# Mixers: ScalarE's copy of the first sequence's turned gated rows, one place forward, in front of the squares of the sixth head

## The chip, the cores and the metric

The kernel runs on one NeuronCore of one Trainium2 chip. The metric is the device time of one execution in microseconds (us); lower is better. The engines named below are TensorE (PE, with its weight loads PEld), VectorE (DVE), ScalarE (ACT), GpSimd (POOL) and SyncE (SP). Each engine works through its own instructions in order and waits for others on semaphores.

## The reference, cut to what matters

The program is a decoder of two layers over 8 sequences of 256 tokens, 512 wide. The part around the change is the second layer's first mixer, a Mamba2 block with four heads, and the cross attention behind it:

```
y = _ssd(x, dt, A, Bm, Cm) + D[None, None, :, None] * x
g = y.reshape(b, l, D_INNER) * jax.nn.silu(z)
gr = g.reshape(b, l, NHEADS, HEADDIM)
rstd = jax.lax.rsqrt(jnp.mean(gr * gr, axis=-1, keepdims=True) + 1e-05)
yn = (gr * rstd).reshape(b, l, D_INNER) * norm_w
return yn @ out_proj_w.T
...
x = x + _L1_attn_ref(_layernorm(x, axis=-1), ...)
x = x + _L1_xattn_ref(_layernorm(x, axis=-1), ctx_2048, ctx_2048, L1_xattn_gamma)
```

Each head's gated rows are squared and summed, scaled by the reciprocal root of their mean square, and all four heads together are multiplied with the output weights. The result, added to `x`, is normalized again and goes into the cross attention.

## The kernel before, in words

The function `mixers` takes the 8 sequences in four pairs, `first` and `second`. Tokens of a sequence lie in two tiles of 128 rows (`NT` is 2, `P` is 128), the 512 columns in four chunks of 128, one for each head (`MH` is 4). The order of each engine's instructions is written out by hand in one block for each engine; semaphores join them. Nothing is planned or scheduled by a program.

The 8 heads of a pair (heads 0 to 3 of the first sequence, 4 to 7 of the second) pass through a loop over `k` on every engine. For one head:

- TensorE's `decays` (L2137 to L2145) builds the decays and the products of B and C in PSUM banks 0 to 3, two of each in turn; `outputs` (L2156 to L2158) multiplies the weights with the inputs.
- ScalarE's `decays` (L1989) takes the exponential of the decays, VectorE's `weights` (L2378) multiplies it with the products, VectorE's `gated` (L2386, L2390) adds the skip and multiplies with the gate and writes `y`.
- ScalarE's `squares` (L1995) squares the head's two row tiles and sums them, GpSimd's `gate_norm` (L1880, L1881) raises the mean to the power of minus a half, and ScalarE's `scaled` (L2004) multiplies `y` with it.

In its round `k` ScalarE issues `decays(k)`, `scaled(k - 3)` and `squares(k - 2)`. The last scaling of a sequence counts `attn_ready` up. TensorE's `turn_gated` (L2096) waits for it, turns 128x128 blocks of `y` by eight multiplications with the identity, into banks 0 and 1, and counts `rowsT_psum` up. Since these banks hold the decays of the last heads, TensorE waits, before it turns the first sequence, until ScalarE has taken the exponential of the eighth head; then it issues `outputs` of the eighth head, and then `project_out(first, j)`:

```
if k == 2 * MH:
    pe.wait_ge(sy["decay_ready"], k0 + k)
    turn_gated(first)
if k >= 1:
    outputs(k0 + k - 1)
...
for j in range(NT):
    project_out(first, j)
turn_gated(second)
project_out(second, 0)
```

ScalarE's `gated_copy` (L1930) copies the turned blocks from banks 0 and 1 into `hT`, one instruction for each bank, and counts `colsT_ready`. `project_out` (the multiplications are in the helper `project_pe`, L188) waits until both copies are done; its first part is the one of the first sequence, for the two row tiles one after the other. Behind it VectorE adds the residual (L2397), takes the statistics (L2301, L2302), GpSimd takes the reciprocal root (L174, L175), VectorE applies it (L2307), ScalarE and VectorE split the rows in two parts (`high` L2010, `low` L2410), and TensorE starts the scores of the cross attention (`scores`, L2178). ScalarE's `context_high(second)` (L1967), a copy of 128x1024, stands between the last scaling of the second sequence and its `gated_copy`. The cross attention takes 32 rounds, and then the next pair begins.

Of the kernel before, what the change touches and what calls it, by code (L numbers as in the profile page):

```python
# [1664 lines left out]
MH = 4  # L1665
# [28 lines left out]
def mixers(nc, sy, const, dr, tiles, nseq=NSEQ):  # L1694
# [3 lines left out]
    with ExitStack() as ctx:  # L1698
# [71 lines left out]
        def dt_calls(p):  # L1770

            n = NT * MH
            return ((0, n), (n, 2 * n)) if p == 0 else ((0, 2 * n),)

        def dt_count(s):

            return s + 1 if s < 2 else s // 2 + 2
# [139 lines left out]
        def _(act):  # L1917
            def rows_copy(s):
                b = s % 2
                for j in range(NT):  # L1920
                    act.wait_ge(sy["rowsT_psum"], 8 * (s // 2) + NT * b + j + 1)
                    act.activation(hT[b][:, :, j * P:(j + 1) * P],
                                   bank(2 * b + j).rearrange("p (c t) -> p c t", c=KC), ACT.Copy
                                   ).then_inc(sy["colsT_ready"], 1)

            def gated_copy(s):
                b = s % 2
                for j in range(NT):
                    act.wait_ge(sy["rowsT_psum"], 8 * (s // 2) + 4 + NT * b + j + 1)
                    act.activation(hT[b][:, :, j * P:(j + 1) * P], bank(j).rearrange("p (c t) -> p c t", c=KC), ACT.Copy  # L1930
                                   ).then_inc(sy["colsT_ready"], 1)

            def time_steps(at, end, count):
                act.wait_ge(sy["dtabs_ready"], count)
                act.activation(dts[:, 2, at:end], dts[:, 1, at:end], ACT.Exp, scale=-1.0).then_inc(sy["dtexp_ready"], 1)
                act.wait_ge(sy["dtone_ready"], count)
                act.activation(dts[:, 4, at:end], dts[:, 3, at:end], ACT.Ln).then_inc(sy["dtln_ready"], 1)

            def convolved(seqs):
                chunks = [NXBC * s + c for s in seqs for c in range(NXBC)]  # L1940
                for n in chunks + [chunks[-1] + 1]:
                    if n <= chunks[-1]:
                        b, c = (n // NXBC) % 2, n % NXBC
                        act.wait_ge(sy["xbc_psum"], n + 1)
                        act.activation(convh[b][:, c, :], bank(1 + n % 3)[:, 0:S], ACT.Identity,
                                       bias=conv_b[:, c:c + 1], scale=conv_w[:, c, 3:4])
                        act.activation(raw[b][:, c, :], bank(1 + n % 3)[:, 0:S], ACT.Copy).then_inc(sy["xbc_raw_ready"], 1)
                    if n > chunks[0]:
                        b, c = ((n - 1) // NXBC) % 2, (n - 1) % NXBC
                        act.wait_ge(sy["conv_ready"], n)  # L1950
                        if n >= 3:
                            act.wait_ge(sy["xbc_ready"], n - 2)
                        act.activation(cth[:, (n - 1) % 2, :], convh[b][:, c, :], ACT.Tanh
                                       ).then_inc(sy["convtanh_ready"], 1)

            def gates(s):
                b = s % 2
                if s >= 2:
                    act.wait_ge(sy[f"mixed_out{b}"], 16 * (s // 2))
                for j in range(NT):  # L1960
                    act.wait_ge(sy["z_psum"], NT * s + j + 1)
                    act.activation(xz[b][:, j, :], bank(4 + 2 * b + j), ACT.Tanh, scale=0.5
                                   ).then_inc(sy["ztanh_ready"], 1)

            def context_high(s):
                act.wait_ge(sy["cx_in"], 16 * (s + 1))
                act.activation(cx2[s % 2][0][:], cx[:], ACT.Copy).then_inc(sy["cx_hi_ready"], 1)  # L1967

            def input_rows(s):
                b = s % 2  # L1970
                act.wait_ge(sy["xrows_psum"], s + 1)
                act.activation(xr[b], bank(4 + b)[:, S:2 * S].rearrange("p (t d) -> p t d", t=NT), ACT.Copy
                               ).then_inc(sy["xrows_ready"], 1)

            def scaled_rows(s):
                b = s % 2
                act.wait_ge(sy["xrows_ready"], s + 1)
                act.wait_ge(sy["dA_ready"], dt_count(s))
                for t in range(NT):
                    for hd in range(MH):  # L1980
                        at = (b * NT + t) * MH + hd
                        ins = act.activation(xdt[b][:, t, hd, :], xr[b][:, t, :], ACT.Copy, scale=dts[:, 8, at:at + 1])
                ins.then_inc(sy["xdt_ready"], 1)

            def decays(k):
                act.wait_ge(sy["decay_psum"], k + 1)
                if k >= 2:
                    act.wait_ge(sy["w_ready"], k - 1)
                act.activation(decay[:, k % 2, :], bank(k % 2)[:, 0:3 * P], ACT.Exp).then_inc(sy["decay_ready"], 1)  # L1989

            def squares(k):
                b, hd = (k // MH) % 2, k % MH
                act.wait_ge(sy["gated_ready"], k + 1)
                for j in range(NT):
                    ins = act.activation(h[b][:, j, hd * P:(hd + 1) * P], y[b][:, j, hd * P:(hd + 1) * P], ACT.Square,  # L1995
                                         accum_out=ssq[b][:, j * MH + hd:j * MH + hd + 1])
                ins.then_inc(sy["sumsq_ready"], 1)

            def scaled(k):
                b, hd = (k // MH) % 2, k % MH  # L2000
                act.wait_ge(sy["gated_norm"], k + 1)
                for j in range(NT):
                    head = y[b][:, j, hd * P:(hd + 1) * P]
                    ins = act.activation(head, head, ACT.Copy, scale=grstd[b][:, j * MH + hd:j * MH + hd + 1])  # L2004
                    if hd == MH - 1:
                        ins.then_inc(sy["attn_ready"], 1)
# [6 lines left out]
            def copy_recips(s, g):  # L2013
                act.wait_ge(sy["recT_psum"], NT * s + g + 1)
                act.activation(y[s % 2][:, g, :], bank(7 - g), ACT.Copy, scale=gamma).then_inc(sy["rec_ready"], 1)
# [20 lines left out]
            for p in range(npair):  # L2036
                first, second = 2 * p, 2 * p + 1
                if p == 0:
                    for s in (first, second):
                        rows_copy(s)  # L2040
                        time_steps(*dt_calls(0)[s], dt_count(s))
                        convolved((s,))
                else:
                    time_steps(*dt_calls(p)[0], dt_count(first))
                    convolved((first, second))
                context_high(first)
                gates(first)
                gates(second)
                input_rows(first)
                input_rows(second)  # L2050
                scaled_rows(first)
                k0 = 2 * MH * p
                for k in range(2 * MH + 3):
                    if k < 2 * MH:
                        decays(k0 + k)
                    if k == 1:
                        scaled_rows(second)
                    if k >= 3:
                        scaled(k0 + k - 3)
                    if 2 <= k < 2 * MH + 2:  # L2060
                        squares(k0 + k - 2)
                    if k == 2 * MH:
                        gated_copy(first)
                context_high(second)
                gated_copy(second)
                for j in range(NT):
                    high(first, j)
                q0 = HP * p
                for i in range(HP + 3):
                    if i < HP:  # L2070
                        exponentials(q0 + i)
                    if 1 <= i <= HP:
                        turned_copy(q0 + i - 1)
                    if i in (8, 9):
                        high(second, i - 8)
                    if i in (11, PAIRS + 11):
                        copy_recips(first + i // PAIRS, 0)
                    if i in (PAIRS + 2, HP + 2):
                        copy_recips(first + i // PAIRS - 1, 1)
                    if p + 1 < npair and i in (HP + 1, HP + 2):  # L2080
                        rows_copy(first + 2 + i - HP - 1)
# [1055 lines left out]
```

## Time and profile before

| what | value |
|---|---|
| time, median of 3 runs | 3378.61 us (3377.27 to 3384.95) |
| span of the profiled execution | 3330.3 us |
| median time less this span | 48.3 us |
| busy share of PE, DVE, ACT, POOL | 92%, 70%, 48%, 24% |

The span goes from the first to the last instruction of one profiled execution. That execution has no device time of its own beside its span here, so the 48.3 us around the span are taken from the median of the three timed runs. Busy shares are averages over stages with different limits. The mixers take the stretch from 1875 to 2656 us of the span; the four pairs' head loops end near 2013, 2198, 2375 and 2546 us.

### The profile page before, as it was taken

How to read it: one execution, taken by the hardware profiler on the slowest of the kernel's cores; microseconds unless marked ns; L12 is line 12 of the kernel's file. 1: busy time of each engine (PE TensorE's matmuls, PEld its weight loads, DVE VectorE, ACT ScalarE, POOL GpSimd, SP SyncE). 2: the span in 40 equal slices, each digit the busy share in tenths (PEclk: the TensorE clock that was granted, in tenths of full speed). 3: DMA queues.
4: the chain of work that ended last, by engine and by line, in shares of the span. 5: the costliest groups of instructions: out<-in, count | busy, mean ns of one | idle time of the engine just before them, and what ended most of it. 6: DMA issues, size and time to landing. Idle time of an engine off the chain costs nothing. (4 is left out here: it accounts for less than half of the span.)

```text
span 3330.3 us, 61582 instructions
## 1 busy us (share of the span) xinstructions
PE 3071.3 (92%) x22897; PEld 2479.2 (74%) x22897; DVE 2317.9 (70%) x4413; ACT 1596.5 (48%) x3648; POOL 805.7 (24%) x1000
## 2 busy tenths in 40 slices
PE   7999999997999799999999769889899889999999
PEld 5666666664888688888888656667576578888888
DVE  4655665564766588888888667868686777777776
ACT  3323333332221455555555336566575655555555
POOL 1221122121554111111111143432323012222222
PEclk9999999998999899999999979999999989999999
DMA  6324332321121677777777621311110132222222
GB/s 260 127 93 148 109 127 102 115 102 39 28 57 34 206 247 241 244 243 240 241 247 248 235 59 58 97 62 54 36 61 7 40 113 78 70 74 73 70 74 70
DMA packets 145099, 401.95 MB, mean 121 GB/s; under 512 B 39200, under 2 KB 48032, under 8 KB 131952
## 3 DMA queue, kind: packets, MB, share of 16 engines
q1 hardware_dynamic: 106448, 323.37, 28.6%
q0 software_dynamic: 18976, 50.45, 5.2%
q10 hardware_dynamic: 19456, 25.18, 2.2%
q8 instruction: 141, 2.31, 0.3%
q14 instruction: 78, 0.64, 0.1%
HBM read 344.16 MB, written 54.76 MB: 120 GB/s over the span
## 5 line engine op out<-in xcount | busy, mean ns | idle before, releaser
L1470 POOL DMA_INDIRECT xg<-normed_rows,idx x128 | 125.4, 979 | 662.5 <-PE psum L1552 590.0
L2655 POOL TENSOR_TENSOR mixf<-act 128x256 f32<-128x256 f32 x128 | 143.5, 1121 | 497.8 <-DVE act L2916 497.8
L174 POOL TENSOR_SCALAR ve<-mv 128x1 f32<-128x1 f32 x112 | 34.9, 311 | 841.0 <-DVE mv L780 575.5
L1567 PE MATMUL psum<-xT_hi,wgu_hi 128*128 128x192 f32 (+1 forms) x1536 | 228.8, 271 | 4.2 <-ACT aT_lo L1534 4.2
L1567 PE MATMUL psum<-xT_lo,wgu_hi 128*128 128x192 f32 (+1 forms) x1536 | 223.2, 268 | 0.0
L1567 PE MATMUL psum<-xT_hi,wgu_lo 128*128 128x192 f32 (+1 forms) x1536 | 223.0, 267 | 0.0
L1606 DVE TENSOR_TENSOR wgu_lo<-wgu,wgu_hi 128x1408 fp32r<-128x1408 f32 x128 | 202.5, 1623 | 22.9 <-ACT wgu_hi L1494 22.8
L1567 PEld LDWEIGHTS psum<-xT_hi,wgu_hi 128*128 128x128 f32 (+1 forms) x1536 | 191.1, 183 | 28.8 <-ACT wgu_hi L1494 21.5
L1507 ACT ACTIVATE eth<-psum 128x192 f32<-128x192 f32 (+1 forms) x192 | 63.2, 329 | 298.7 <-PE psum L1567 298.7
L2024 ACT ACTIVATE scratch<-psum,smin 128x512 f32<-128x512 f32 x256 | 173.7, 685 | 62.8 <-DVE smin L2416 60.6
L1567 PEld LDWEIGHTS psum<-xT_lo,wgu_hi 128*128 128x128 f32 (+1 forms) x1536 | 190.8, 183 | 0.0
L1567 PEld LDWEIGHTS psum<-xT_hi,wgu_lo 128*128 128x128 f32 (+1 forms) x1536 | 190.7, 183 | 0.0
L2416 DVE TENSOR_REDUCE smin<-psum 128x2 f32<-128x1024 f32 x128 | 155.4, 1217 | 34.0 <-PE psum L2178 33.2
L1494 ACT ACTIVATE wgu_hi<-wgu 128x1408 fp32r<-128x1408 f32 x128 | 169.5, 1379 | 18.7 <-DMA wd<-in_w_d_dram 18.7
L2916 DVE TENSOR_TENSOR act<-act,maskT 128x512 f32<-128x512 f32 x128 | 88.2, 689 | 116.9 <-ACT act L2693 116.9
L2188 PEld LDWEIGHTS psum<-ident,scratch 128*128 128x128 f32 x1024 | 108.9, 141 | 59.4 <-issue 38.2
L2188 PE MATMUL psum<-ident,scratch 128*128 128x128 f32 x1024 | 144.8, 281 | 8.1 <-DVE scratch L2423 4.9
L1640 DVE SCALAR_TENSOR_TENSOR eact<-eth,psum 128x192 f32<-128x192 f32 (+1 forms) x192 | 67.5, 352 | 108.9 <-ACT eth L1507 107.1
L2926 DVE TENSOR_TENSOR ca_lo<-act,ca_hi 128x512 fp32r<-128x512 f32 x128 | 134.4, 1050 | 12.5
L558 PE MATMUL psum<-hT_hi,w_slot 128*128 128x256 f32 x768 | 113.5, 292 | 12.3 <-ACT hT_hi L468 5.9
L1053 POOL DMA_INDIRECT slot_token<-tok_i,slot_w x96 | 102.5, 1068 | 77.3 <-DVE slot_r L1337 52.2
L902 DVE TENSOR_SCALAR arena<-psum,hi 128x512 f32<-128x512 f32 x128 | 87.3, 745 | 43.9 <-PE psum L672 43.9
(431 smaller groups left out, 8681.1 us busy)
## 6 DMA issues: line engine op xcount, KB each, us to landing
wgu<-in_w_gu_dram SPq DMA_DIRECT2D x64, 1408.0 KB, 6.1
w_slot<-w_split SPq DMA_DIRECT2D x21, 2048.0 KB, 7.8
wd<-in_w_d_dram SPq DMA_DIRECT2D x64, 512.0 KB, 8.7
w_raw<-in_w_dram SPq DMA_DIRECT2D x128, 256.0 KB, 2.6
expert_out<-yo ACTq DMA_DIRECT2D x64, 256.0 KB, 5.2
w_slot<-w_split SPq DMA_DIRECT2D x28, 512.0 KB, 4.9
wd<-in_w_d_dram SPq DMA_DIRECT2D x64, 192.0 KB, 9.0
w_split<-w_slot SPq DMA_DIRECT2D x4, 2048.0 KB, 9.0
```

The costliest lines, as they stand in the source:

```text
L558: ins = pe.matmul(out, lhs_of(lp, kc), rhs_of(rp, kc), start=(m == 0 and kc == 0), stop=(m == 2 and kc == KC - 1))
L1053: pool.indirect_dma_start(out=dr["slot_token"], out_offset=bass.IndirectOffsetOnAxis(ap=slot_w[s % 2][:, j, k:k + 1], axis=0), in_=tok_i[s ...
L1470: pool.indirect_dma_start(out=xg[b][0:w, t, :], out_offset=None, in_=rows, in_offset=bass.IndirectOffsetOnAxis(ap=idx[b][0:w, t:t + 1], ax ...
L1494: act.activation(wgu2[b][0][:, gu], wgu[b][:, gu], ACT.Copy).then_inc(sy["wgu_hi"], 1)
L1567: ins = pe.matmul(bank(2 + m)[0:w, gu * CAP:(gu + 1) * CAP], wgu2[b][wp][:, gu, kc, m0:m0 + w], xT2[b][xp][:, kc, :], start=(i == 0 and kc ...
L1606: dve.tensor_tensor(wgu2[b][1][:, gu], wgu[b][:, gu], wgu2[b][0][:, gu].bitcast(F32), ALU.subtract).then_inc(sy["wgu_lo"], 1)
L2024: act.activation(prob[:, q % 4, k, :], bank_pair(2 * (q % 2))[:, k, :], ACT.Exp, bias=smin[b][:, n, k:k + 1], scale=-1.0, accum_out=ssum[b ...
L2188: ins = pe.transpose(bank(4 + k)[:, mc * P:(mc + 1) * P], prob[:, q % 4, k, mc * P:(mc + 1) * P], ident)
L2416: dve.tensor_reduce(smin[(q // PAIRS) % 2][:, q % PAIRS, :], bank_pair(2 * (q % 2)), AX.X, ALU.min).then_inc(sy["smin_ready"], 1)
L2655: pool.tensor_tensor(mixf[:, g % LAG, :], act2[:, g % LAG, 0, :], act2[:, g % LAG, 1, :], ALU.add).then_inc(sy["f_mix"], 1)
L2916: dve.tensor_tensor(act2[:, g % LAG], act2[:, g % LAG], maskT[(g // FC) % 2][:, 2:4, :], ALU.mult).then_inc(sy["f_ca"], 1)
L2926: dve.tensor_tensor(ca2[1][:, g % LAG], act2[:, g % LAG], ca2[0][:, g % LAG].bitcast(F32), ALU.subtract).then_inc(sy["f_ca_lo"], 1)
```

## The change

ScalarE's `gated_copy(first)` moves in the last rounds of the head loop. It stood in round `k == 8` behind `scaled` of head 5 and `squares` of head 6 (heads counted from 0). It now stands in round `k == 7`, behind `scaled` of head 4 and ahead of `squares` of head 5, the sixth head. No instruction is added or removed, and no other engine's order is touched.

```diff
                     if k >= 3:
                         scaled(k0 + k - 3)
+                    if k == 2 * MH - 1:
+                        gated_copy(first)
                     if 2 <= k < 2 * MH + 2:
                         squares(k0 + k - 2)
-                    if k == 2 * MH:
-                        gated_copy(first)
                 context_high(second)
                 gated_copy(second)
```

On ScalarE, at the end of the first pair's head loop, the order changes as follows (the same piece stands in each of the four pairs; L1989 is `decays`, L2004 `scaled`, L1995 `squares`, L1930 `gated_copy`):

```order
 L1989 ACTIVATE decay<-psum 128x384
 L2004 ACTIVATE y<-y,grstd 128x128 x2
-L1995 ACTIVATE h,ssq<-y 128x128 x2
-L2004 ACTIVATE y<-y,grstd 128x128 x2
-L1995 ACTIVATE h,ssq<-y 128x128 x2
 L1930 ACTIVATE hT<-psum 128x4x128 x2
+L1995 ACTIVATE h,ssq<-y 128x128 x2
+L2004 ACTIVATE y<-y,grstd 128x128 x2
+L1995 ACTIVATE h,ssq<-y 128x128 x2
 L2004 ACTIVATE y<-y,grstd 128x128 x2
 L1995 ACTIVATE h,ssq<-y 128x128 x2
```

The copy passes two pairs of squarings and one pair of scalings.

On TensorE, which waits for this copy and is waited for by it, the same place in the first pair reads thus before and after alike (L2096 is `turn_gated`, L2156 to L2158 `outputs` of the eighth head, L188 `project_out`, L2178 the first scores):

```order
L2096 MATMUL psum<-ident,y 128x128 x8
L2156 MATMUL psum<-scratch,wgt 128x128
L2157 MATMUL psum<-scratch,wgt 128x128
L2158 MATMUL psum<-scratch,wgt 128x128
L188 MATMUL psum<-w_mo,hT 128x512 x8
L2096 MATMUL psum<-ident,y 128x128 x8
L188 MATMUL psum<-w_mo,hT 128x512 x4
L2178 MATMUL psum<-cx_hi,h_hi 128x512 x2
```

Nothing moved here. The profile counts each of these L188 multiplications twice (16 and 8 records), and the three of L2156 to L2158 as six.

## Rows read from the trace of the kernel before

**Rows 1.** The page's head and its busy line.

```profile
span 3330.3 us, 61582 instructions
PE 3071.3 (92%) x22897; PEld 2479.2 (74%) x22897; DVE 2317.9 (70%) x4413; ACT 1596.5 (48%) x3648; POOL 805.7 (24%) x1000
```

**Rows 2.** Line L1930: who waited for the copies, all pairs.

```profile
L1930 ACT ACTIVATE hT<-psum x16: 572/584/597, 2016.1 to 2560.9; 128x512 f32<-128x512 f32 x16
...
  PE psum L188: 19.0, 8
```

**Rows 3.** Timeline, first pair: start, length, engine, line, [idle before, releaser].

```profile
2011.42 1.09 PE L2096 MATMUL psum<-ident,y 128*128 128x128 f32 x8 [1.15 <-ACT decay L1989]
...
2012.08 0.69 ACT L2004 ACTIVATE y<-y,grstd 128x128 f32<-128x128 f32 x2 [0.71 <-POOL grstd L1881]
...
2012.80 0.39 PE L2158 MATMUL psum<-scratch,wgt 128*128 128x128 f32 x2
...
2013.03 0.31 ACT L1995 ACTIVATE h<-y 128x128 f32<-128x128 f32 x1 [0.26 <-DVE y L2390]
...
2014.90 0.69 ACT L2004 ACTIVATE y<-y,grstd 128x128 f32<-128x128 f32 x2 [1.17 <-POOL grstd L1881]
2015.50 0.29 ACT L1995 ACTIVATE h<-y 128x128 f32<-128x128 f32 x1
...
2016.08 1.05 ACT L1930 ACTIVATE hT<-psum 128x512 f32<-128x512 f32 x2
...
2016.54 0.69 POOL L1881 TENSOR_TENSOR grstd<-ssq,minus_half 128x2 f32<-128x2 f32 x1
...
2017.19 9.91 PE L188 MATMUL psum<-w_mo,hT 128*128 128x512 f32 x16 [4.01 <-ACT hT L1930]
2017.26 0.69 ACT L2004 ACTIVATE y<-y,grstd 128x128 f32<-128x128 f32 x2
```

**Rows 4.** Windows, first pair: stretch; busy by engine; PEclk.

```profile
2015.00:2016.00 1.00, 0.00 (x0) 0.00 (x0) 0.09 (x1) 1.00 (x6) 0.00 (x0) 0.99 0.00 0
2016.00:2017.20 1.20, 0.01 (x1) 0.01 (x1) 0.00 (x0) 1.14 (x4) 0.85 (x2) 0.50 0.00 0
2017.20:2022.20 5.00, 5.00 (x6) 2.17 (x7) 0.00 (x0) 2.92 (x9) 0.90 (x3) 0.50 0.02 3
2024.00:2026.50 2.50, 2.50 (x7) 1.07 (x6) 0.39 (x1) 0.00 (x0) 0.00 (x0) 1.00 0.00 0
```

**Rows 5.** Timeline, first pair, behind the gap: the second sequence's way.

```profile
2019.62 0.69 ACT L2004 ACTIVATE y<-y,grstd 128x128 f32<-128x128 f32 x2 [1.08 <-POOL grstd L1881]
...
2020.22 1.04 ACT L1967 ACTIVATE cx_hi<-cx 128x1024 fp32r<-128x1024 f32 x1
...
2026.93 1.04 PE L2096 MATMUL psum<-ident,y 128*128 128x128 f32 x8
...
2027.57 1.08 ACT L1930 ACTIVATE hT<-psum 128x512 f32<-128x512 f32 x2 [6.31 <-PE psum L2096]
...
2028.71 3.70 PE L188 MATMUL psum<-w_mo,hT 128*128 128x512 f32 x8 [0.74 <-ACT hT L1930]
...
2031.14 1.48 DVE L2410 SCALAR_TENSOR_TENSOR h_lo<-h,h_hi 128x512 fp32r<-128x512 f32 x2
...
2032.34 0.52 PE L2178 MATMUL psum<-cx_hi,h_hi 32*128 32x512 f32 x4
```

**Rows 6.** Timeline of PE, pairs two and four, first projection and the turning behind it.

```profile
2201.95 9.69 PE L188 MATMUL psum<-w_mo,hT 128*128 128x512 f32 x16 [4.01 <-ACT hT L1930]
2211.48 1.04 PE L2096 MATMUL psum<-ident,y 128*128 128x128 f32 x8
...
2550.30 9.59 PE L188 MATMUL psum<-w_mo,hT 128*128 128x512 f32 x16 [4.01 <-ACT hT L1930]
2559.73 1.04 PE L2096 MATMUL psum<-ident,y 128*128 128x128 f32 x8
```

**Rows 7.** Windows at the start of pairs two and three, columns as in rows 4.

```profile
2132.00:2134.00 2.00, 2.00 (x11) 2.00 (x12) 0.00 (x0) 0.00 (x0) 0.51 (x1) 0.51 0.02 2
2312.00:2314.00 2.00, 2.00 (x11) 1.77 (x10) 0.40 (x3) 1.97 (x4) 0.25 (x1) 1.00 0.05 4
```

**Rows 8.** Timeline of VectorE's first two weights, pairs three and four.

```profile
2354.08 1.01 DVE L2378 TENSOR_TENSOR wgt<-decay,psum 128x384 f32<-128x384 f32 x2
2359.80 0.56 DVE L2378 TENSOR_TENSOR wgt<-decay,psum 128x384 f32<-128x384 f32 x1 [4.70 <-PE psum L2145]
...
2527.45 1.02 DVE L2378 TENSOR_TENSOR wgt<-decay,psum 128x384 f32<-128x384 f32 x2 [2.55 <-ACT decay L1989]
2530.84 0.55 DVE L2378 TENSOR_TENSOR wgt<-decay,psum 128x384 f32<-128x384 f32 x1 [2.37 <-PE psum L2145]
```

## The prediction

> **What bounds the kernel now.** I read the page first: TensorE is busy for 92% of the span and no other engine for more than 70% [rows 1]. An average over 3330 us says little of a change at four places, so the next view is the line of the copy itself. TensorE waited 19.0 us in eight waits for the copies of L1930 [rows 2]. The timelines split this sum: four waits of 4.01 us for the first sequence's copy [rows 3, 6] and four of 0.74 us for the second's [rows 5], 16.04 + 2.96 = 19.0 us. So the places to look at are the four gaps of 4.01 us.
>
> The timeline around the first gap shows what TensorE lacks. It has turned the rows by 2012.51 (2011.42 + 1.09) and ended the eighth head's outputs by 2013.19 (2012.80 + 0.39). The copy of the turned rows starts only at 2016.08, not because its input is late, but because it stands in ScalarE's queue behind the squares of head 5, its scaling, and the squares of head 6; and that scaling itself stood 1.17 us for GpSimd's power [rows 3]. The projection starts at 2017.19.
>
> The gap has a second price. The granted clock was full until about 2016.0, 2.8 us after the last matmul, and then 0.50, the 1.2 GHz level; it was still 0.50 from 2017.2 to 2022.2, under dense matmuls, and full again from 2024 [rows 4]. In the first pair the 16 records of the projection take 2026.93 - 2017.19 = 9.74 us from its start to the next turning [rows 3, 5]. The same multiplication at the full clock, 8 records of the second sequence, takes 2032.34 - 2028.71 = 3.63 us to the scores that follow it [rows 5]. Twice that is 7.26 us and counts the start and end of a group twice; I take 7.1 us for 16. So the slow clock costs 9.74 - 7.1 = 2.6 us in pair one. In pairs two and four the stretch is 9.53 and 9.43 us [rows 6] (pair three repeats pair two), 2.4 and 2.3 us over 7.1.
>
> **The change part by part.** Nothing is removed or added: two copies of 584 ns in each pair [rows 2], issued earlier.
>
> *When the copy can start.* It now stands behind the scaling of head 4, which starts at 2012.08. When nothing is waited for, ScalarE's next instruction follows a pair of scalings after 0.60 us (2014.90 to 2015.50) [rows 3], so the copy comes up at 2012.68. Its input: for the second sequence the first copy starts 0.64 us after the turning starts (2026.93 to 2027.57) [rows 5], here 2011.42 + 0.64 = 2012.06, and the last turning ends by 2012.51. Both banks are thus ready and I put the wait at nothing. From the other side: if the second bank follows the first by half of the turning (0.55 us), it is ready at 2012.06 + 0.55 = 2012.61, which is still ahead of 2012.68.
>
> *When the projection can start.* From the copies' start to the projection are 2017.19 - 2016.08 = 1.11 us [rows 3]. 2012.68 + 1.11 = 2013.79, instead of 2017.19: 3.40 us earlier. The eighth head's outputs end at 2013.19, so TensorE is free, and its gap shrinks from 4.01 to 0.60 us.
>
> *The clock.* A gap of 0.60 us behind a stretch in which the clock stayed full through gaps of 1.15 us [rows 3] should leave it full: 2.6 us in pair one on top, and the turning of the second sequence can start at 2013.79 + 7.1 = 2020.9 instead of 2026.93.
>
> *What is pushed back.* The squares of head 5 waited for VectorE until 2013.03. They now stand behind the copies, which hold ScalarE for about 1.0 us (they last 1.05 us together, and a following instruction starts a little before the end), that is until 2013.68: 0.65 us late. Behind them are queued: GpSimd's power for head 5, the scaling of head 5, the squares of head 6, and so on to the scaling of head 7 and the context copy. The copy no longer stands between the squares of head 6 and the scaling that now starts at 2017.26, but nothing is won there, since GpSimd's power ends at 2016.54 + 0.69 = 2017.23 anyway [rows 3]. So the 0.65 us stay: the scaling of head 7 starts at 2020.27 instead of 2019.62 and ends at about 2020.96, the context copy starts at 2020.87 instead of 2020.22 and ends at 2021.91 [rows 5]. TensorE turns from 2020.9; its first four blocks need only the first of the two scaled tiles, so this delay, if it shows, is under 0.1 us. Before, it had about 6.6 us of slack.
>
> *What is late next.* The second sequence's copy waits for the turning (2020.9 + 0.64 = 2021.5) and for ScalarE, which is in the context copy until 2021.9. So it starts at 2021.9, held by ScalarE, instead of 2027.57: 5.67 us earlier. Its projection follows 1.14 us later, as before (2027.57 to 2028.71) [rows 5]: 2023.0 for 2028.71. Of the 2.6 us that the clock gives, 0.35 us are thus lost again to the context copy.
>
> *What follows.* The scores start when this projection ends, if the split rows are there. Before, the second part of the split starts by the end of the first at about 2031.88 (2031.14 and half of 1.48), 0.46 us ahead of TensorE's 2032.34 [rows 5]. That chain hangs on the first sequence's projection, which ends 3.40 + 2.6 = 6.0 us earlier, so its slack grows to 0.8 us. The scores start 5.7 us earlier, and from there on everything, the 32 rounds and the next pair, hangs on these starts and moves along. GpSimd's gathers and the loads are started by counts of the same loop.
>
> *The sum.* In pair one the copy starts 2021.9 - 2017.19 = 4.71 us after the projection's old start; before it started 10.38 us after it (2027.57 - 2017.19). In the other pairs the old figure is the turning's start and 0.64 us: 9.53 + 0.64 = 10.17 twice, 9.43 + 0.64 = 10.07 [rows 6]. The gains are 5.67 + 5.46 + 5.46 + 5.36 = 21.95 us. The span goes from 3330.3 to 3308.3 us. The median of the runs shown is 48.3 us above the span, and I keep that distance: 3378.6 - 22.0 = 3356.6 us.
>
> *What the shift may do elsewhere.* The clock also falls at other places, and not in each pair. At the start of pair two it was 0.51, at the same place of pair three 1.00 [rows 7]; and from the first weights of the head loop to the third are 2359.80 - 2354.08 = 5.72 us in pair three and 2530.84 - 2527.45 = 3.39 us in pair four, which kept its clock [rows 8]. So one such fall costs up to 2.3 us, and a shift by some us can make or save it.
>
> A rule of the skill bears on this. The Trainium skill, page "TensorE: Matmul & The Clock Gate", section "What's actually happening", says that the monitor behind the gate runs freely, so that where the clock changes depends on when the work arrives, not only on what it is. The differences between pairs in rows 7 and 8 agree. By that rule the shift can cost or give several us at places that the change does not touch; what that would make here is the third rival below.
>
> **The rivals.**
>
> *The clock falls all the same.* The transposes and short heads ahead of the gap may count for too little. For it: it fell in all four pairs. Against it: it stayed full through 1.15 us gaps, and fell only 2.8 us after the last matmul. Then the gain is the 3.40 us of the gap alone, carried through turning and copy: 13.6 us, 3365.0 us. Chance 9%.
>
> *The rounds behind do not move.* If the end of a pair were set by something that the copy does not start, such as the gathers or the context's low part on GpSimd, the gap's gain would be waited away: 3378.6 us. Against it: GpSimd is busy 24% [rows 1] and its work there is started by the rounds' own counts. Chance 4%.
>
> *The clock falls elsewhere more often.* At 2.3 us each [rows 8], three falls more take 6.9 us back: 15.1 us of gain, 3363.5 us. Two falls fewer give 4.6 us on top: 3352.0 us. Chance of a shift of 3 us or more either way 15%, still faster.
>
> *ScalarE stands at the copy.* The other side. The copy now heads the queue of squares, scalings and the context copy; if the turned rows came late, all of these and the second sequence's turning would wait. What TensorE waits for before it turns is the exponential of the eighth head, which ScalarE issues ahead of the scaling of head 4, so the wait worked out is nothing. It decides only from a wait of about 6 us on, where the slack of 6.6 us of the second's turning is used up; a wait of 8 us would cost about 2 us a pair: 3386 us. Chance 3%.
>
> **How the numbers follow.** The forecast as worked out, within 3 us, has 69%; the rivals have 9, 4, 15 and 3%. The predicted time is 3356.6 us. The range reaches to the better bound, 3351, and takes in the rival of the clock, 3365, with a margin: 3351 to 3366. A measurement of this kernel tells 0.2%, 6.8 us, from no change. Only the second rival and part of small remainders end within that: 4%; slower 3%; faster 93%.
>
> **What would show it right or wrong.** In the profile after: the L188 waits for L1930 sum to about 4 x 0.6 + 4 x 1.1 = 7 us instead of 19.0. The first projection begins about 0.6 us behind the outputs of the eighth head, and its 16 records show no 0.50 clock. The second's copy begins right behind the context copy, without idle time. The scaling of head 7 is 0.65 us later against the exponential of head 7. ScalarE's idle time before the first copy is nothing. If the clock row shows 0.50 behind the shorter gap, or ScalarE idles before the first copy, that step was wrong; if all of these hold and the span is not about 22 us shorter, the loss lies in the rounds behind or in falls of the clock at other places.

## The result, and the profile after

| | kernel before | changed kernel |
|---|---|---|
| median | 3379.99 us (3377.27 to 3384.95, 4 runs) | 3353.63 us (3351.07 to 3361.1, 4 runs) |
| ratio | | 0.9923, 95% interval 0.9911 to 0.9935 |

The change makes the kernel 26.4 us faster by the medians, 22 to 30 us by the interval. The forecast was 22.0 us.

The first pair in the trace of the changed kernel, timeline, to be laid beside [rows 3] and [rows 5]:

```profile
2023.37 1.09 PE L2096 MATMUL psum<-ident,y 128*128 128x128 f32 x8 [1.15 <-ACT decay L1989]
2024.02 0.69 ACT L2004 ACTIVATE y<-y,grstd 128x128 f32<-128x128 f32 x2 [0.71 <-POOL grstd L1881]
2024.62 1.06 ACT L1930 ACTIVATE hT<-psum 128x512 f32<-128x512 f32 x2
...
2025.58 0.30 ACT L1995 ACTIVATE h<-y 128x128 f32<-128x128 f32 x1
2025.74 7.13 PE L188 MATMUL psum<-w_mo,hT 128*128 128x512 f32 x16 [0.61 <-ACT hT L1930]
...
2027.41 0.69 ACT L2004 ACTIVATE y<-y,grstd 128x128 f32<-128x128 f32 x2 [1.15 <-POOL grstd L1881]
...
2032.13 0.69 ACT L2004 ACTIVATE y<-y,grstd 128x128 f32<-128x128 f32 x2 [1.08 <-POOL grstd L1881]
2032.71 1.04 PE L2096 MATMUL psum<-ident,y 128*128 128x128 f32 x8
2032.73 1.04 ACT L1967 ACTIVATE cx_hi<-cx 128x1024 fp32r<-128x1024 f32 x1
...
2033.68 1.06 ACT L1930 ACTIVATE hT<-psum 128x512 f32<-128x512 f32 x2
2034.79 3.70 PE L188 MATMUL psum<-w_mo,hT 128*128 128x512 f32 x8 [1.05 <-ACT hT L1930]
...
2036.92 1.47 DVE L2410 SCALAR_TENSOR_TENSOR h_lo<-h,h_hi 128x512 fp32r<-128x512 f32 x2
...
2038.42 0.52 PE L2178 MATMUL psum<-cx_hi,h_hi 32*128 32x512 f32 x4
```

The copy starts 0.60 us behind the scaling of head 4, without idle time. TensorE's gap is 0.61 us instead of 4.01. The 16 records of the projection take 2032.71 - 2025.74 = 6.97 us to the next turning instead of 9.74. The second copy starts right behind the context copy. From the first turning to the scores are 15.05 us instead of 20.92.

The waits of TensorE for the copies are 6.6 us instead of 19.0 [rows 2]:

```profile
  PE psum L188: 6.6, 8
```

The windows of the same stretch, columns as in [rows 4], show the clock full throughout:

```profile
2025.00:2028.00 3.00, 2.39 (x8) 1.07 (x7) 1.97 (x8) 1.85 (x8) 0.95 (x2) 1.00 0.00 0
2028.00:2033.00 5.00, 5.00 (x15) 2.31 (x14) 0.78 (x2) 2.83 (x14) 1.76 (x4) 1.00 0.00 0
```

Worked out in the same way for each pair, first turning to first scores, in us:

| pair | before | changed | difference |
|---|---|---|---|
| 1 | 20.92 | 15.05 | 5.87 |
| 2 | 20.70 | 15.06 | 5.64 |
| 3 | 20.71 | 15.05 | 5.66 |
| 4 | 20.61 | 15.06 | 5.55 |

Together 22.7 us. This takes the first trace of the kernel before as the measure; a second trace of it (`base`, below) has 81.1 us at the four places where the first has 82.9, and against it the gain is 20.8 us. The rest of the trace cannot be compared so simply: the changed kernel's profiled execution has a longer span (3359.1 us) than the one of before [rows 1], though the changed kernel is faster by the clocked runs. The section on the hardware comes back to this.

### The profile page after: what moved, and what is told of

Read it like the earlier page. It is cut to its first block and busy times, and to the rows that moved or that the text cites. A ratio compares the mean times of both kernels' runs of the same rounds, so it can differ in the third digit from the quotient of the medians.

```text
span 3359.1 us, 61582 instructions
## 1 busy us (share of the span) xinstructions
PE 3100.1 (92%) x22897; PEld 2500.8 (74%) x22897; DVE 2317.4 (69%) x4413; ACT 1596.6 (48%) x3648; POOL 801.4 (24%) x1000
## 5 line engine op out<-in xcount | busy, mean ns | idle before, releaser
L2188 PE MATMUL psum<-ident,scratch 128*128 128x128 f32 x1024 | 154.1, 292 | 10.1 <-issue 4.7
L558 PE MATMUL psum<-hT_hi,w_slot 128*128 128x256 f32 x768 | 113.1, 291 | 12.2 <-ACT hT_hi L468 5.8
```

The source lines that it names most:

```text
L2188: ins = pe.transpose(bank(4 + k)[:, mc * P:(mc + 1) * P], prob[:, q % 4, k, mc * P:(mc + 1) * P], ident)
```

## The experiments

Four sets of runs were made, and each is compared with runs of the kernel before on its own device: medians 3331.90 us (the first four kernels), 3331.91 us (the next four), 3382.02 us (`control`, `heads23`, `ctx23`), 3388.25 us (`base`). The second set has no run of the changed kernel itself, so its kernels are laid beside it by the ratio. "Local" is the sum over the four pairs of the stretch from turning to scores, against the 82.9 us of before.

| kernel | median us | ratio to before, 95% interval | local us |
|---|---|---|---|
| `again` | 3314.26 | 0.9945, 0.9932 to 0.9959 | -22.7 |
| `warm` | 3325.94 | 0.9983, 0.9974 to 0.9992 | -10.3 |
| `behind` | 3319.66 | 0.9967, 0.9955 to 0.9979 | -20.1 |
| `ctx` | 3312.37 | 0.9942, 0.9928 to 0.9955 | -24.0 |
| `gapback` | 3333.54 | 1.0002, 0.9992 to 1.0013 | -4.0 |
| `early` | 3313.08 | 0.9933, 0.9915 to 0.9952 | -22.7 |
| `split` | 3313.48 | 0.9941, 0.9926 to 0.9956 | -26.1 |
| `heads` | 3318.14 | 0.9954, 0.9937 to 0.9971 | -22.7 |
| `control` | 3355.73 | 0.9930, 0.9914 to 0.9946 | -22.7 |
| `heads23` | 3355.64 | 0.9927, 0.9913 to 0.9941 | -22.7 |
| `ctx23` | 3352.94 | 0.9921, 0.9907 to 0.9935 | -24.0 |
| `base` | 3387.44 | 0.9996, 0.9981 to 1.0012 | -1.9 |

**`again`**: the changed kernel, unchanged.

> The changed kernel once more. Theory (the four gaps and the clock inside them): the stretch from the first turning to the second sequence's projection is 11.4 us in each pair, as in its first trace, against 17.29, 17.07, 17.08 and 16.97 us before, 22.7 us in all, and the time is 22 to 23 us under the kernel before. Rival (the change also gives something elsewhere, since 3353.6 against 3380.0 us is 26.4 us): the time is 25 us or more under it again, and the trace shows further stretches of the mixers that are shorter. The 2060 to 2068 us stretch of the first trace, where TensorE, VectorE and ScalarE stood idle behind a fetch, either comes back (then it belongs to the new order) or does not.

The four places are 15.06 us each, as in the first trace. The gain is 17.6 us by the medians, 13.7 to 22.7 us by the interval: smaller than the first time, and less than the 22 to 23 us expected. The idle stretch at 2060 us did not come back.

**`warm`**: the order of before, and work of no use in TensorE's gap.

```diff
+                for n in range(4):
+                    pe.matmul(bank(2), ident, w_mo[:, n, :], start=True, stop=True)
                 for j in range(NT):
                     project_out(first, j)
```

> The kernel before, with the copy in its old place, and four multiplications of no use by TensorE in the gap of 4.01 us, so that its clock is kept. Theory (the gap costs twice, by itself and by the clock behind it): the gap keeps its end, the projection's 16 records take 7.0 us instead of 9.4 to 9.7, and the time is about 10 us under the kernel before (2.8 + 2.6 + 2.6 + 2.5). Rival (the clock is no part of it, or falls all the same): no change, within 2 us.

The timeline of TensorE in pair one (L2261 is the filling):

```profile
2014.27 1.09 PE L2096 MATMUL psum<-ident,y 128*128 128x128 f32 x8 [1.15 <-ACT decay L1989]
...
2015.86 3.60 PE L2261 MATMUL psum<-w_mo,ident 128*128 128x512 f32 x8
2020.04 7.13 PE L188 MATMUL psum<-w_mo,hT 128*128 128x512 f32 x16 [0.58 <-ACT hT L1930]
2027.01 1.04 PE L2096 MATMUL psum<-ident,y 128*128 128x128 f32 x8
```

The projection starts 5.77 us behind the turning, exactly as before, and yet takes 6.97 us instead of 9.74. So the low clock behind the gap came from the gap, and filling it takes 10.3 us off the four places. The time fell by 3 to 9 us, less than that. Against the second trace of before, whose four places are 1.9 us shorter, the local gain is 8.5 us, which the interval (up to 8.7 us) still holds. The mechanism holds; whether part of its gain is given back elsewhere is not shown by this run alone.

**`behind`**: the copy one place later than in the changed kernel.

```diff
                     if 2 <= k < 2 * MH + 2:
                         squares(k0 + k - 2)
-                    if k == 2 * MH:
+                    if k == 2 * MH - 1:
                         gated_copy(first)
```

> The copy one place later than in the changed kernel, behind the squares of head 5 and ahead of round 8. Theory: the first copy starts 0.9 us later than in the changed kernel, TensorE's gap is 1.5 us, its clock stays full, the squares of head 5 are not pushed back, and the second sequence's copy is held by the turning, no more by the context copy: 0.6 us a pair, 2.4 us in all slower than the changed kernel, about 20 us under the kernel before. Rival (the clock falls behind a gap of 1.5 us): about 12 us under the kernel before.

```profile
2013.72 1.09 PE L2096 MATMUL psum<-ident,y 128*128 128x128 f32 x8 [1.15 <-ACT decay L1989]
2014.38 0.69 ACT L2004 ACTIVATE y<-y,grstd 128x128 f32<-128x128 f32 x2 [0.71 <-POOL grstd L1881]
...
2015.93 1.06 ACT L1930 ACTIVATE hT<-psum 128x512 f32<-128x512 f32 x2
...
2017.05 7.13 PE L188 MATMUL psum<-w_mo,hT 128*128 128x512 f32 x16 [1.56 <-ACT hT L1930]
```

As expected: a gap of 1.56 us, and still 6.97 us for the projection, so the clock stays full. Locally it is 2.6 us behind the changed kernel. By the times it is 5.4 us behind `again`, more than the local difference, and only 12.2 us under the kernel before (7 to 15 us by the interval), where about 20 were expected. That is the figure of the rival, the fall of the clock, though the trace shows none at the four places: the time alone would have named the wrong cause. It is also the clearest case of a local gain (20.1 us, or 18.2 us against `base`) that the time does not show in full.

**`ctx`**: the context copy behind the second gated copy.

```diff
-                context_high(second)
                 gated_copy(second)
+                context_high(second)
```

> The changed kernel with ScalarE's context copy of the second sequence moved behind the second sequence's gated copy. Theory: the second copy then waits for the turning alone and starts 0.33 us earlier in each pair, 1.3 us in all. Rival (the context copy is then late for what follows, or the split rows hold the scores): no change or slower.

The second copy waits 0.51 us for the turning now and TensorE 0.74 us for the copy instead of 1.05, in each pair. The local gain is 1.3 us; the medians differ by 1.9 us, which the intervals don't tell apart from nothing.

**`gapback`**: ScalarE's order is the changed one, TensorE waits again.

```diff
+                pe.wait_ge(sy["sumsq_ready"], k0 + 2 * MH - 1)
                 for j in range(NT):
                     project_out(first, j)
```

> The changed kernel, with TensorE made to wait, ahead of the first sequence's projection, for the squares of head 6 (their count as GpSimd takes it). ScalarE's order stays the changed one. Theory (only TensorE's start counts, and the clock hangs on the gap): the gap is back at about 3.7 us, the projection's records are at the half clock again at their start, the four places are about 3 + 2.6 us longer each, and the time is that of the kernel before, within 3 us. Rival (the new order on ScalarE is worth something by itself): at least 5 us under the kernel before.

In pairs one and two (timeline of TensorE):

```profile
2017.33 10.12 PE L188 MATMUL psum<-w_mo,hT 128*128 128x512 f32 x16 [3.61 <-ACT h L1995]
2027.29 1.04 PE L2096 MATMUL psum<-ident,y 128*128 128x128 f32 x8
...
2206.51 8.83 PE L188 MATMUL psum<-w_mo,hT 128*128 128x512 f32 x16 [3.62 <-ACT h L1995]
2215.18 1.04 PE L2096 MATMUL psum<-ident,y 128*128 128x128 f32 x8
```

The windows show that in pair one the clock is low from the projection's start on, and that in pair two it fell later than the projection's start, at about 2207.7:

```profile
2017.40:2023.20 5.80, 5.80 (x7) 2.45 (x8) 0.00 (x0) 2.92 (x9) 1.72 (x4) 0.50 0.01 3
...
2206.00:2207.50 1.50, 0.98 (x3) 0.51 (x4) 0.00 (x0) 0.46 (x4) 0.87 (x2) 1.00 0.00 0
2207.50:2210.00 2.50, 2.50 (x5) 1.03 (x4) 0.00 (x0) 1.37 (x7) 0.89 (x3) 0.54 0.00 0
```

So a gap of 3.62 us costs 8.67 - 6.97 = 1.7 us of clock here and 9.96 - 6.97 = 3.0 us in pair one of the same execution: how much is lost depends on how much of the projection runs at the low clock. In the other two pairs it is 1.7 and 1.5 us, so the 2.6 us expected were reached in pair one alone, and the four places together are 4.0 us shorter than before. The time is that of the kernel before, within 0.13% either way, so nearly the whole gain hangs on TensorE's earlier start; the new order on ScalarE shows no worth by itself.

**`early`**: the copy ahead of the scaling of head 4.

```diff
-                    if k >= 3:
-                        scaled(k0 + k - 3)
                     if k == 2 * MH - 1:
                         gated_copy(first)
+                    if k >= 3:
+                        scaled(k0 + k - 3)
```

> The copy one more place forward, ahead of the scaling of head 4, so that ScalarE stands at it until TensorE has turned the rows. Theory: ScalarE stands about 0.7 us, the first projection begins 0.5 us earlier than in the changed kernel, the squares of head 5 come no later than there, and the second sequence's copy, held by the scalings and the context copy, does not move: the same time as the changed kernel, within 1 us. Rival (the wait at the head of ScalarE's queue is paid by all behind it): 3 us or more slower than the changed kernel.

```profile
2015.25 1.09 ACT L1930 ACTIVATE hT<-psum 128x512 f32<-128x512 f32 x2 [0.75 <-PE psum L2096]
2016.22 0.69 ACT L2004 ACTIVATE y<-y,grstd 128x128 f32<-128x128 f32 x2
2016.39 7.13 PE L188 MATMUL psum<-w_mo,hT 128*128 128x512 f32 x16
```

ScalarE stands 0.75 us at the copy, TensorE's gap is gone, and what is won there is lost again at the second turning, which waits 0.25 us for the last scaling, and at the second copy behind the context copy (TensorE 1.11 us instead of 1.05). The sum is 15.06 us, as in the changed kernel. A wait at the head of ScalarE's queue costs nothing here.

**`split`**: as `ctx`, and each half of a projection waits only for its own copy.

```diff
-                pe.wait_ge(sy["colsT_ready"], 8 * (s // 2) + 4 + NT * (b + 1))
+                pe.wait_ge(sy["colsT_ready"], 8 * (s // 2) + 4 + NT * b + j + 1)
```

> The context copy behind the second gated copy, and each half of a projection waits only for the copy of its own row tile. Theory: the first projection begins 0.48 us earlier, the turning of the second sequence is then held by the last scaling (0.13 us earlier), the second projection begins 0.6 us earlier than with the context copy moved alone, and 0.9 us earlier than in the changed kernel, in each pair: 3.8 us under the changed kernel. Rival (the gain is taken back by falls of the clock elsewhere or by the split rows): within 1 us of the changed kernel.

Locally 14.20 us for each pair, 0.86 us under the changed kernel, 3.4 us in all, close to the 3.8 expected. The ratio, 0.9941, is beside the 0.9942 of `ctx` and the 0.9945 of `again`: no gain that the times tell.

**`heads`**: TensorE's idle time at each head loop's start filled with a product computed over again.

```diff
+                for n in range(8 if k % (2 * MH) == 1 else 1):
-                pe.matmul(prod[:, 0:2 * P], xbc[b][:, 1, 0:P], xbc[b][:, 2 + hd, :], start=True, stop=True)
+                    pe.matmul(prod[:, 0:2 * P], xbc[b][:, 1, 0:P], xbc[b][:, 2 + hd, :], start=True, stop=True)
```

> The changed kernel, with the product of B and C of the second head of each pair computed seven times over on top, in TensorE's idle time of 3.7 us at the start of the head loop (3 us of work). Theory (falls of the clock at other places take back some of the gain): no 0.50 clock at the head starts of pairs two and three, from first to third weights 3.4 us instead of 5.0, and up to 3 us under the changed kernel, less what falls still elsewhere. Rival (those falls hide behind VectorE): the same time as the changed kernel.

The falls at the head starts of pairs two and three are gone. The time is not better. The design was poor: in the trace of `again` TensorE's idle time there is 3.72 us in pairs two and three and only 0.66 and 0.78 us in pairs one and four, where most of the 3 us of filling is paid: from first to third weights these pairs take 5.52 and 5.40 us instead of 3.39. The run says nothing on the question, so it was made again without these two.

**`control`, `heads23`, `ctx23`**: the changed kernel; it with the filling for `k in (2 * MH + 1, 4 * MH + 1)` alone; and this with the context copy moved.

> The changed kernel as the measure for the two others of this batch. Theory: 17 to 19 us under the kernel before, 22.7 us at the four places less 4 to 5 us at others. Rival (what was lost elsewhere in its second measurement was chance): 22 us or more.

> The products of the second head computed seven times over on top in pairs two and three alone, where TensorE stood idle for 3.7 us; in pairs one and four it had only 0.7 us and the filling cost more than it gave. Theory (a fall of the clock at a head start is paid in full): no 0.50 clock at the head starts of pairs two and three, 5.0 and 4.7 us from first to third weights become 3.4 us, 3 us under the changed kernel. Rival (the fall then comes at another place): within 1 us of the changed kernel.

> The same filling, with the context copy behind the second gated copy. Theory: the two gains add, 3 + 1.3 us under the changed kernel. Rival: no more than 2 us under it.

VectorE's first and third weights at pair two, in `control` and then in `heads23`:

```profile
2194.02 1.01 DVE L2378 TENSOR_TENSOR wgt<-decay,psum 128x384 f32<-128x384 f32 x2
2198.96 0.56 DVE L2378 TENSOR_TENSOR wgt<-decay,psum 128x384 f32<-128x384 f32 x1 [3.93 <-PE psum L2145]
```

```profile
2196.10 1.01 DVE L2379 TENSOR_TENSOR wgt<-decay,psum 128x384 f32<-128x384 f32 x2
2199.48 0.55 DVE L2379 TENSOR_TENSOR wgt<-decay,psum 128x384 f32<-128x384 f32 x1 [2.38 <-PE psum L2146]
```

4.94 us became 3.38 us, and in pair three 4.46 us became 3.39: the fall at a head start costs 1.1 to 1.6 us there, and keeping TensorE busy removes it. Yet the medians are 3355.73 and 3355.64 us: 2.6 us won at two places don't show in the time. But the six times of `control` reach from 3349.7 to 3364.2 us, so a gain of this size would not show either, and the runs do not decide between theory and rival. In the trace of `heads23` the clock is low at 2492 to 2499 and 2512 to 2516 us, in `control` at 2509 to 2517 us, so the falls elsewhere are not the same in the two traces. `ctx23` is 2.8 us under `control` by the medians, with overlapping intervals. It has the lowest ratio of all, 0.9921, and is not shown to beat the changed kernel.

`control` itself is 26.3 us under the kernel before on its device by the medians, 18 to 29 us by the interval. The theory, 17 to 19 us, missed this; the rival, that the loss elsewhere in `again` was chance, comes nearer, and the interval still holds both.

**`base`**: the kernel before, for a second trace.

> The kernel before, unchanged, for a second trace of it. Theory: the four places are as in its first trace (20.6 to 20.9 us from turning to scores, four gaps of 4.01 us, the clock low behind them), and the clock's other falls stand at other places than in the first trace; the time is within 2 us of the kernel before. Rival: the four places themselves differ from the first trace.

The gaps are 4.01 us again, in all four pairs. The projections behind them take 9.83, 8.67, 9.48 and 8.38 us, where the first trace had 9.74, 9.53, 9.53 and 9.43. So the stretches from turning to scores are 21.00, 19.84, 20.66 and 19.56 us: only one lies in the expected 20.6 to 20.9, and for the clock's part the rival was right. Pair two:

```profile
2242.13 8.83 PE L188 MATMUL psum<-w_mo,hT 128*128 128x512 f32 x16 [4.01 <-ACT hT L1930]
2250.80 1.04 PE L2096 MATMUL psum<-ident,y 128*128 128x128 f32 x8
```

So the gaps are the same to 0.01 us in two executions, and what the clock adds behind them is 1.4 to 2.9 us a pair.

## Why the prediction was right

The mechanism held, and so did its size at the four places. The agreement for the whole program is in part luck: 26.4 us were measured against 22.0 forecast, but the same change measured 17.6 us (`again`) on a device whose median before is 3331.9 us and 26.3 us (`control`) on one with 3382.0. Point by point:

- *When the copy can start*: 0.60 us behind the scaling, no wait for the turning. Measured 0.60 and none.
- *When the projection can start*: 1.11 us behind the copies' start, a gap of 0.60 us. Measured 1.12 and 0.61.
- *The clock*: full through the shorter gap. Measured 1.00 in all windows of the stretch. The projection took 6.97 us, where I had put 7.1 us. These 0.13 us gave nothing, since ScalarE's context copy, not the turning, held the second copy.
- *What is pushed back*: the squares of head 5 were to come 0.65 us late. They start 1.56 us behind the scaling of head 4, before 0.95 us [rows 3]: 0.61 us late. The scaling of head 7 starts 8.11 us behind that scaling, before 7.54 us [rows 3, 5]: 0.57 us late. TensorE came to turn at 2032.71, with no idle time ahead of it; the pair of scalings ends at 2032.82, and the first blocks need only the first of the two.
- *What is late next*: the second copy, held by the context copy. It starts with no idle time ahead of it, and `ctx`, which puts the context copy behind it, gains 0.3 us in each pair.
- *What follows*: the second part of the split was to be 0.8 us ahead of TensorE. It starts at about 2037.66 (2036.92 and half of 1.47), 0.76 us ahead of the scores at 2038.42, so the split did not hold them.
- *The sum*: 21.95 us forecast at the four places, 22.7 us in the trace, about 0.19 us more in each pair. In pair one the second copy starts 10.31 us behind the first turning instead of the 10.48 worked out: the delay on ScalarE was 0.57 us instead of 0.65, and the copy follows the context copy's start by 0.95 us instead of 1.04; its projection follows after 1.11 us instead of 1.14. The measured gain was 22 to 30 us in the first comparison, 14 to 23 and 18 to 29 us in the later two. The first and the third hold 22.7 us and the second ends there; 22.0 us lies in all three, at the lower end of the first.
- *The rivals*: the clock did not fall behind the gap; the rounds moved along; ScalarE did not stand at the copy, and `early`, where it does, loses nothing. The third rival, falls that move elsewhere, is not excluded. The clock does fall at other places in different executions, and `behind` took 20.1 us off the four places (18.2 against `base`) and 7 to 15 us off the time.

Where such microseconds go can be read by taking the local stretch off the distance from one pair's turning to the next. `ctx` has the changed order as `again` has it, and `gapback` nearly the four places of before:

| without the local stretch, us | before | `again` | `ctx` | `gapback` |
|---|---|---|---|---|
| start to pair 1 | 2011.42 | 2015.90 | 2008.61 | 2011.96 |
| pair 1 to 2 | 163.85 | 164.32 | 164.20 | 168.44 |
| pair 2 to 3 | 156.77 | 157.82 | 157.80 | 155.48 |
| pair 3 to 4 | 150.16 | 154.80 | 151.85 | 151.83 |
| pair 4 to the end | 765.16 | 763.52 | 764.87 | 767.56 |

The first row ends ahead of the first copy that is moved. The program up to there is the same in all four, and yet it differs by up to 7.3 us: single executions differ by that much without any change.

In `again` 4.6 us come back between pairs three and four, in `ctx` 1.7 us. The clock's cost there has this size. These are windows of 25 us at that place, in the first trace of before, in `again` and in `ctx`:

```profile
2478.00:2503.00 25.00, 24.15 (x198) 21.53 (x199) 16.91 (x41) 15.58 (x36) 9.75 (x15) 1.00 0.12 43
2463.00:2488.00 25.00, 23.85 (x207) 20.11 (x206) 13.74 (x32) 12.31 (x27) 4.39 (x9) 0.80 0.12 44
2463.00:2488.00 25.00, 25.00 (x160) 22.11 (x159) 17.05 (x43) 14.48 (x32) 14.28 (x22) 0.93 0.13 43
```

A granted clock of 0.80 over 25 us takes 5.0 us of TensorE's work, 0.93 takes 1.75 us. One of the two falls in `again`, finer, at the start of pair four:

```profile
2475.00:2477.00 2.00, 2.00 (x22) 2.00 (x19) 1.30 (x2) 1.09 (x2) 0.00 (x0) 1.00 0.47 139
2477.00:2479.00 2.00, 2.00 (x16) 2.00 (x15) 0.00 (x0) 0.00 (x0) 0.00 (x0) 0.73 0.90 369
2479.00:2481.00 2.00, 2.00 (x9) 1.82 (x9) 0.52 (x3) 0.40 (x2) 0.00 (x0) 0.50 0.06 25
```

So what comes back there is paid to the clock. That the falls are caused by the shift is not shown: `ctx` has the same order and only one of them, and the second trace of before, on another device, has a fall in that region too, at 2529 to 2536 us. `gapback`, with the long gap back, takes 7.4 us more than the first trace of before in the last four rows together, `again` 4.5 us. This speaks for a lucky first trace of before rather than for falls that the new order makes, but whether the order makes such falls more frequent stays open.

One thing I had wrong, without harm to the forecast: the 48.3 us between span and median. I read it as time around the span. An execution's own time is 2 us above its span (3361.1 and 3359.1 us for the profiled one of the changed kernel). The rest of the 48 us fits the difference between devices: the kernel before has medians of 3331.9, 3382.0 and 3388.3 us on three of them; on which device its first trace was taken is not on record. As the sum was a difference, it survived.

## What to carry to other kernels

A copy that is ready but queued behind work with slack is found by laying the start of the copy beside the end of its input, not by any busy share: here ScalarE was busy 48% and still set TensorE's start. Price a gap on TensorE twice, once for itself and once for the records behind it that run at the half clock; a filled gap (`warm`) separates the two. And don't expect local gains to come out to the microsecond in the whole: the same change gave 17.6 and 26.3 us on two devices with 22.7 us in both traces, and falls of the clock elsewhere differ from trace to trace. Where two kernels differ by under 3 us in the trace, these times did not tell them apart.

## What the runs showed of the hardware

The same program differs by up to 56 us from device to device (medians 3331.9 to 3388.3 us), and part of it lies in stalls such as this one. In the second trace of before (`base`), windows of 2066 to 2081 us, and what VectorE and TensorE waited for:

```profile
2066.00:2071.00 5.00, 3.20 (x47) 2.11 (x44) 2.65 (x4) 3.11 (x9) 3.79 (x4) 1.00 1.01 400
2071.00:2076.00 5.00, 3.45 (x11) 1.51 (x12) 0.00 (x0) 0.00 (x0) 2.83 (x3) 0.57 0.89 275
2076.00:2081.00 5.00, 5.00 (x36) 3.53 (x39) 4.18 (x7) 3.57 (x9) 0.94 (x1) 0.50 0.30 88
...
2069.39 0.27 PE L2209 MATMUL psum<-scratch,cxT 128*32 128x128 f32 x1 [1.01 <-issue]
2076.78 1.23 DVE L2416 TENSOR_REDUCE smin<-psum 128x2 f32<-128x1024 f32 x1 [7.41 <-remote]
```

TensorE's matmuls come one by one with idle time put down to issue, VectorE stands for 7.4 us and ScalarE for 7.0, and the clock falls. It is not one stall but three: the cross attention behind each of the first three pairs has one. VectorE's idle time there is 7.4, 6.7 and 8.1 us in `base`, 6.6, 6.6 and 7.3 us in the first trace of the changed kernel, 6.7, 7.3 and 6.6 us in `control`, and `heads23` and `ctx23`, on the device of `control`, have three each as well. None of the nine other traces has any: the eight from the two devices with medians of 3331.9 us, and the first trace of before, whose span of 3330.3 us fits such a device. So the stalls belong to neither order.

They stand where the DMA engines move 400 GB/s, but that rate alone is not the cause. In `again` they move 401 GB/s at the same place of the program, and TensorE is busy throughout:

```profile
2050.00:2055.00 5.00, 5.00 (x64) 3.50 (x60) 4.15 (x7) 4.21 (x12) 3.79 (x4) 1.00 1.02 401
```

What else differs between the devices is not shown. The three stalls, about 21 us at VectorE, are part of the reason why the changed kernel's first trace has a longer span than the first of before; it is also 12.0 us later at its first turning, ahead of all of them.

The clock behind gaps of the same length is not the same: after 4.01 us the projection took between 8.38 and 9.83 us in eight instances, and after 0.6 to 1.56 us always 6.97 us. The Trainium skill, page "TensorE: Matmul & The Clock Gate", section "What's actually happening", says that the monitor runs freely, so that the point of a change varies with the arrival of work; the eight instances agree with it.
